# S4D convolution on one core: one table for both sides of the state, and the odd chunk sums as three split products

## The chip, the cores and the metric

One Trainium2 chip, one of its cores. The metric is the device time of one execution in microseconds. The kernel before takes 853.24 us (median of three runs, 852.15 to 855.84).

## The reference, cut to what matters

```python
dtA = (-exp(log_A_real) + 1j * A_imag) * exp(log_dt)[:, None]           # 128 channels x 64 modes
Cs = C * (exp(dtA) - 1.0) / A
K = 2.0 * einsum('hn,hnl->hl', Cs, exp(dtA[:, :, None] * arange(2048))).real
y = irfft(rfft(u * mask) * rfft(K))[..., :2048] + u * mask * D[:, None]  # u: 64 batches x 128 x 2048
x = x + y * mask                                                         # mask: t < length[b]
```

For each channel, 64 sequences of 2048 samples go through a causal convolution whose kernel is a sum of 64 damped complex exponentials. The work is fp32.

## The kernel before

A **prologue** builds tables of powers of the exponentials for all channels. Then comes one **slot per channel**, 128 of them. Slots 0 to 11 and 120 to 127 are written out; the 108 between run in a hardware loop, six to a turn, where semaphore values and table addresses stand in registers. No scheduler places anything: each engine runs its own `slot(g, j)` in the order in which it is written, and semaphores tie the engines together. In slot h, `here` is channel h, `one`, `two` and `three` are h+1, h+2 and h+3, `back` is h-1.

**Per channel.** A sequence is cut into 8 chunks of 256 samples, each an even and an odd block of 128. `turn_x` (L1006) transposes x on TensorE: four transposes for the even blocks into the PSUM bank xt_even, four for the odd ones into xt_odd. ScalarE copies xt_even to `uhi` (rounded to fp32r) and xt_odd to `uod` (full fp32); VectorE forms the remainder `ulo` (`x_low`). `chunk_sums` (L1025 to L1039) gives what each of the first 7 chunks adds to the 128 state rows (64 real, 64 imaginary) for 7 x 64 = 448 columns: three fp32r products for the even block (hi by hi, hi by lo, lo by hi; lines 1021 to 1023) and one fp32 product with `eod` for the odd block (L1038), which the trace shows as two matmuls. It raises `s_in`.

**The scan.** The states follow from the sums by products with powers of the exponential in `RV`. ScalarE writes a copy with the halves swapped (`turn_odds`, `turn_pairs`, `turn_evens`: two ACTIVATEs each into `room`), and VectorE does two instructions for each step (`mid`, then v in place; L911), in `pairs`, `fours` and `odds`. `z_high` on ScalarE and `z_low` on VectorE split the finished states into `zhi` and `zlo`.

**Outputs.** `toep_even` and `toep_odd` (L1067) are the products within a chunk, with the Toeplitz rows `traw` that SyncE's queue reads from the DRAM tensor krows, split by `thi` and `tlo`. `from_state` adds zhi, zlo by the table `fhi`, `flo`, three fp32r products of 256 columns for each of four pieces, and raises `s_y` after the second and the fourth. It waits for `s_zlo` and `s_flo` before the first. `choose` (L900) then writes y into the x tile under the mask, and SyncE's queue stores it.

**Tables E and F.** For each channel, GpSimd's `channel` forms 2 x 256 columns by two products of W and B (L520, L521) and a difference (L529): half 0 is turned by `turn_e` and gives ehi, elo, eod, half 1 gives fhi, flo. W holds two families of powers, X for E and Y for F, both made in the prologue by `level` (six instructions for a doubling) on VectorE.

**The order that matters here.** TensorE: sums of `one`, `turn_x` of `two`, Toeplitz products of `here` with `turn_e` of `two` in the middle, `from_state` of `here`. VectorE: `choose` of `back` twice, `odds` of `here`, `pairs` of `one`, `z_low` of `here`, `x_low` and `e_low` of `two`, `fours` of `one`. So within a slot `z_low(here)` stands behind `pairs(one)`, which waits for the sums of the same slot; and `from_state(here)`, later in that slot, waits for `z_low(here)`.

## Time and profile before

| | us |
|---|---|
| profiled execution, its own time | 853.14 |
| its span, first to last instruction | 851.3 |
| start of the Toeplitz products of slot 0 | 51.4 |
| TensorE busy | 816.7 (96%) |
| VectorE, GpSimd, ScalarE busy | 730.0, 641.3, 619.2 |
| granted TensorE clock, mean | 0.999 |

Busy time is the union of an engine's records. TensorE's records overlap, since a matmul's ends are modelled and the next one streams while it drains: the pace is read from start to start. A row of the timeline gives start, duration, engine, line, operation, what is written and read, how many records are merged, and in brackets the idle time before it with its releaser.

### The profile page before, as it was taken

How to read it: one execution, taken by the hardware profiler on the slowest of the kernel's cores; microseconds unless marked ns; L12 is line 12 of the kernel's file. 1: busy time of each engine (PE TensorE's matmuls, PEld its weight loads, DVE VectorE, ACT ScalarE, POOL GpSimd, SP SyncE). 2: the span in 40 equal slices, each digit the busy share in tenths (PEclk: the TensorE clock that was granted, in tenths of full speed). 3: DMA queues.
4: the chain of work that ended last, by engine and by line, in shares of the span. 5: the costliest groups of instructions: out<-in, count | busy, mean ns of one | idle time of the engine just before them, and what ended most of it. 6: DMA issues, size and time to landing. Idle time of an engine off the chain costs nothing.

```text
span 851.3 us, 22217 instructions
## 1 busy us (share of the span) xinstructions
PE 816.7 (96%) x6168; PEld 752.9 (88%) x6168; DVE 730.0 (86%) x2020; ACT 619.2 (73%) x1717; POOL 641.3 (75%) x708
## 2 busy tenths in 40 slices
PE   0799999999999999999999999999999999999997
PEld 0779998989999999999998999999999999999996
DVE  7878988888888888888888888888888888888886
ACT  4777776777777777777777777777777777777774
POOL 5887776777777878787787878777787877778771
PEclk9999999999999999999999999999999999999999
DMA  5235877777777787777877777777777877777875
GB/s 108 50 74 145 197 189 183 192 186 184 190 187 199 185 193 192 185 197 184 196 185 193 191 186 197 184 195 185 194 191 190 196 184 195 185 194 189 197 191 137
DMA packets 161391, 152.69 MB, mean 179 GB/s; under 512 B 13656, under 2 KB 161240, under 8 KB 161240
## 3 DMA queue, kind: packets, MB, share of 16 engines
q1 hardware_dynamic: 161064, 152.15, 72.5%
q10 hardware_dynamic: 304, 0.26, 0.1%
q8 instruction: 11, 0.18, 0.1%
q14 instruction: 12, 0.10, 0.0%
HBM read 84.02 MB, written 67.30 MB: 178 GB/s over the span
## 4 chain that ended last, share of the span: by engine, by line
PE 89%; DVE 4%; DMA 3%; ACT 1%; SPq 1%; issue 1%; DVEq 0%
PE y L1021 13%; PE y L1023 13%; PE y L1022 13%; PE y L1067 13%; PE v L1038 11%; PE xt_even L1006 6%; PE xt_odd L1006 6%; PE v L1021 3%; PE v L1022 3%; DMA xall<-in_x_dram 3%; PE v L1023 3%; PE y L1016 2%; PE y L1017 2%; SPq L355 1%; ACT room L542 0%
## 5 line engine op out<-in xcount | busy, mean ns | idle before, releaser
L542 ACT ACTIVATE room<-v 64x192 f32<-64x192 f32 (+1 forms) x768 | 235.8, 307 | 171.9 <-DVE v L911 156.0
L911 DVE SCALAR_TENSOR_TENSOR v<-v,RV,mid 128x192 f32<-128x192 f32 (+2 forms) x512 | 192.3, 376 | 55.0
L911 DVE SCALAR_TENSOR_TENSOR mid<-room,RV,v 128x192 f32<-128x192 f32 (+2 forms) x512 | 184.3, 360 | 42.1 <-ACT room L542 23.5
L1021 PE MATMUL y<-thi,uhi 128*128 128x256 f32 x511 | 186.0, 364 | 0.0
L900 DVE COPY_PREDICATED xall<-mask,y 128x512 f32<-128x512 int32 x254 | 174.4, 735 | 1.7 <-issue 1.7
L1021 PE MATMUL y<-fhi,zhi 128*128 128x256 f32 x511 | 154.3, 302 | 1.3 <-DVE zlo L735 1.2
L1023 PE MATMUL y<-thi,ulo 128*128 128x256 f32 x511 | 144.2, 282 | 0.0
L1023 PE MATMUL y<-fhi,zlo 128*128 128x256 f32 x511 | 143.8, 281 | 0.0
L1022 PE MATMUL y<-tlo,uhi 128*128 128x256 f32 x511 | 143.7, 281 | 0.0
L1022 PE MATMUL y<-flo,zhi 128*128 128x256 f32 x511 | 143.7, 281 | 0.0
L521 POOL TENSOR_TENSOR room<-W,B 128x512 f32 (+1 forms) x127 | 141.7, 1116 | 0.0
L520 POOL TENSOR_TENSOR room<-W,B 128x512 f32 (+1 forms) x127 | 134.8, 1061 | 3.0 <-DVE W L873 2.8
L1067 PE MATMUL y<-traw,uod 128*128 128x128 f32 x680 | 130.4, 273 | 0.0
L1006 PEld LDWEIGHTS xt_even<-ident,xall 128*128 128x128 f32 x512 | 63.3, 142 | 56.8 <-issue 46.9
L503 POOL TENSOR_TENSOR flo<-pf,fhi 128x256 fp32r<-128x256 f32 x64 | 46.7, 730 | 79.0 <-ACT fhi L542 79.0
L1067 PEld LDWEIGHTS y<-traw,uod 128*128 128x128 f32 x680 | 104.8, 189 | 0.0
L503 POOL TENSOR_TENSOR flo<-room,fhi 128x256 fp32r<-128x256 f32 x64 | 46.7, 729 | 73.8 <-ACT fhi L542 73.8
L1022 PEld LDWEIGHTS y<-tlo,uhi 128*128 128x128 f32 x511 | 98.1, 192 | 0.2 <-issue 0.2
L1021 PEld LDWEIGHTS y<-thi,uhi 128*128 128x128 f32 x511 | 97.4, 191 | 0.9 <-POOL tlo L508 0.7
L1021 PEld LDWEIGHTS y<-fhi,zhi 128*128 128x128 f32 x511 | 96.5, 189 | 1.7 <-issue 1.7
L1022 PEld LDWEIGHTS y<-flo,zhi 128*128 128x128 f32 x511 | 96.7, 189 | 0.0
L1023 PEld LDWEIGHTS y<-fhi,zlo 128*128 128x128 f32 x511 | 96.5, 189 | 0.0
(195 smaller groups left out, 1939.6 us busy)
## 6 DMA issues: line engine op xcount, KB each, us to landing
xall<-in_x_dram SPq DMA_DIRECT2D x256, 256.0 KB, 4.6
out_dram<-xall SPq DMA_DIRECT2D x254, 256.0 KB, 3.4
traw<-krows SPq DMA_DIRECT2D x128, 128.0 KB, 3.0
NXY<-B SPq DMA_DIRECT2D x2, 512.0 KB, 6.2
krows<-ksb SPq DMA_DIRECT2D x8, 1.0 KB, 2.2
krows<-ksb SPq DMA_DIRECT2D x8, 4.0 KB, 3.6
krows<-ksb SPq DMA_DIRECT2D x8, 11.0 KB, 4.0
out_dram<-xall SPq DMA_DIRECT2D x1, 128.0 KB, 2.5
```

Source lines behind the costliest of these rows:

```text
L503: pool.tensor_tensor(flo[j % 2][:], pf[j % 2][:, 1, ::-1], fhi[j % 2][:].bitcast(F32), ALU.subtract).then_inc(s_flo, 1)
L520: pool.tensor_tensor(tw1[:], w1, b1, ALU.mult).then_inc(s_gpa, 1)
L521: pool.tensor_tensor(tw2[:], w2, b2, ALU.mult).then_inc(s_gpa, 1)
L542: return act.activation(dst, src, ACT.Copy)
L900: dve.copy_predicated(xs[j][:, a:a + 512], mask[:, a:a + 512], yb[j % 2][part][:]).then_inc(s_pred, 1)
L911: return dve.scalar_tensor_tensor(out=out, in0=src, scalar=RV[:, k:k + 1, h], in1=other, op0=ALU.mult, op1=ALU.add)
L1006: mm = pe.transpose(xt[par][:, c * P:(c + 1) * P], xs[j][:, b * BLK:(b + 1) * BLK], ident[:])
L1021: pe.matmul(o, a_hi, b_hi, start=start, stop=False, skip_group_check=True)
L1022: pe.matmul(o, a_hi, b_lo, start=False, stop=False, skip_group_check=True)
L1023: return pe.matmul(o, a_lo, b_hi, start=False, stop=stop, skip_group_check=True)
L1038: pe.matmul(v, eod[k][:], uod[j % 3][:, cols], start=False, stop=True, skip_group_check=True).then_inc(s_in, 1)
L1067: mm = pe.matmul(y_cols(g, j, c)[:, BLK:2 * BLK], uod[j % 3][:, b], traw[k][:, :BLK - 1:-1], start=False, stop=False, skip_group_check=True)
```

## The change

**One table.** The starting values of X and Y are changed so that E and F are the same table: X starts at half the root of the modulus of z = Y(1) times lambda, with its sign and phase; the prologue gets the products for z (GpSimd), two squares and a square root (ScalarE), a reciprocal and five small operations (VectorE). The states are then multiplied by a factor for each mode, kept as a seventh row of `RV` (step S): `z_high` gets a per-partition scale, `z_low` becomes a SCALAR_TENSOR_TENSOR. GpSimd forms 256 columns instead of 512. VectorE's levels are made for Y (levels 0 to 2), then X (0 to 3), then Y's last, where before each of the first three did both; the prologue's transposes go through 3 PSUM banks instead of 5, and ScalarE alone takes them.

**Odd sums.** E is split over its whole width (`ehi`, `elo` with 256 columns). `x_odd` makes a second copy `uoh` (fp32r, 448 columns), GpSimd forms its remainder `uol` (`odd_low`). `chunk_sums` becomes `even_sums` and `odd_sums`, three fp32r products each.

**Order.** On TensorE the sums of `one` have the odd transposes of `two` between them, and the even transposes, now of `three`, stand in the middle of `from_state`. The other engines' slots are reordered as the diff shows. SyncE's queue loads x four slots ahead instead of three and stores before it loads `traw`.

```diff
-BANKS = 5
+BANKS = 3
 
 
 STEPS = [("R", 0), ("R", 1),
-         ("B1", 12), ("B2", 12), ("X1", 12), ("X2", 12), ("Y1", 12), ("Y2", 12),
-         ("B1", 8), ("B2", 8), ("X1", 8), ("X2", 8), ("Y1", 8), ("Y2", 8),
-         ("Y1", 0), ("Y1", 4), ("Y2", 0), ("Y2", 4),
-         ("B1", 0), ("B1", 4), ("B2", 0), ("B2", 4),
-         ("X1", 0), ("X1", 4), ("X2", 0), ("X2", 4)]
+         ("B1", 12), ("B2", 12), ("Y1", 12), ("Y1", 8), ("B1", 8), ("B2", 8),
+         ("X1", 12), ("X2", 12), ("X1", 8), ("X2", 8), ("X1", 0), ("X1", 4), ("X2", 0), ("X2", 4),
+         ("B1", 0), ("B1", 4), ("B2", 0), ("B2", 4), ("Y1", 0), ("Y1", 4), ("S", 0)]
 T_K = len(STEPS)
...
-        W2 = sb("W2", [P, 2, SQ, H])
+        W2 = sb("W2", [P, SQ, H])
...
-        ehi = [sb(f"ehi{i}", [P, P], F32R) for i in range(2)]
-        elo = [sb(f"elo{i}", [P, P], F32R) for i in range(2)]
-        eod = [sb(f"eod{i}", [P, P]) for i in range(2)]
-
-        tw1, tw2 = (room[:, i].rearrange("p (a b c) -> p a b c", a=2, b=SQ) for i in (5, 6))
-        pf = [sb("pf0", [P, 2, CHUNK]), room[:, 7].rearrange("p (a q) -> p a q", a=2)]
+        ehi = [sb(f"ehi{i}", [P, 2 * P], F32R) for i in range(2)]
+        elo = [sb(f"elo{i}", [P, 2 * P], F32R) for i in range(2)]
+        uoh = [sb(f"uoh{i}", [P, EVERY], F32R) for i in range(2)]
+        uol = [sb(f"uol{i}", [P, EVERY], F32R) for i in range(2)]
+
+        tw1, tw2 = (room[:, i, 0:CHUNK].rearrange("p (b c) -> p b c", b=SQ) for i in (5, 6))
+        pf = [sb("pf0", [P, CHUNK])[:], room[:, 7, 0:CHUNK]]
         fhi = [sb(f"fhi{i}", [P, CHUNK], F32R) for i in range(2)]
...
-                start = isinstance(g, int) and g == 0
                 early = isinstance(g, int) and g < 2
-                if exists(g, j, 3) and not (start and j + 3 < SLOTS):
-                    if exists(g, j, -3):
-                        sp.wait_ge(s_out[(j + 3) % SLOTS], 32 * on(g, j, 3)[0])
-                    load_x(*on(g, j, 3))
+                if exists(g, j, 4) and not (early and h + 4 < SLOTS):
+                    sp.wait_ge(s_out[(j + 4) % SLOTS], 32 * on(g, j, 4)[0])
+                    load_x(*on(g, j, 4))
...
+                if exists(g, j, -1):
+                    sp.wait_ge(s_pred, 2 * h)
+                    store(*on(g, j, -1))
                 if exists(g, j, 2):
                     sp.wait_ge(s_intra, h + 1)
                     load_t(*on(g, j, 2))
-                if exists(g, j, -1):
-                    sp.wait_ge(s_pred, 2 * h)
-                    store(*on(g, j, -1))
...
+            def table(g, j):
+
+                h = chan(g, j)
+                w1 = W1[:, 0, h, :].unsqueeze(2).broadcast_to([P, SQ, SQ])
+                w2 = W2[:, :, h].unsqueeze(2).broadcast_to([P, SQ, SQ])
+                b1 = B1[:, h, :].unsqueeze(1).broadcast_to([P, SQ, SQ])
+                b2 = B2[:, h, :].unsqueeze(1).broadcast_to([P, SQ, SQ])
...
+                pool.tensor_tensor(tw1, w1, b1, ALU.mult).then_inc(s_gpa, 1)
+                pool.tensor_tensor(tw2, w2, b2, ALU.mult).then_inc(s_gpa, 1)
...
+            def odd_low(g, j):
+
+                h = chan(g, j)
+                pool.wait_ge(s_uod, h + 1)
+                pool.wait_ge(s_uoh, h + 1)
+                if exists(g, j, -2):
+                    pool.wait_ge(s_in, h - 1)
+                pool.tensor_tensor(uol[j % 2][:], uod[j % 3][:, 0:EVERY], uoh[j % 2][:].bitcast(F32),
+                                   ALU.subtract).then_inc(s_uol, 1)
...
+                f_low(*here)
+                if not exists(g, j, -1):
+                    t_low(*here)
+                if has2 and exists(g, j, -1):
+                    difference(*two)
+                if has1:
+                    odd_low(*one)
+                if has2 and not exists(g, j, -1):
+                    difference(*two)
+                if exists(g, j, -1):
+                    t_low(*here)
+                if has3:
+                    table(*three)
...
+                if exists(g, j, -2):
+                    act.wait_ge(s_in, chan(g, j) - 1)
+                copy(uoh[j % 2][:], xt[1][:, 0:EVERY]).then_inc(s_uoh, 1)
...
+            act.wait_ge(s_z, 1)
+            act.activation(sq_re, z_re, ACT.Square)
+            act.activation(sq_im, z_im, ACT.Square).then_inc(s_sq, 1)
...
+            take(("B1", 12), ("Y1", 12))
+            act.wait_ge(s_n2, 1)
+            act.activation(m0, n2, ACT.Sqrt).then_inc(s_m0, 1)
...
-                copy(ehi[j % 2][:], e_bank(j)[:, 0:P]).then_inc(s_ehi, 1)
-
-            def e_odd(g, j):
-                copy(eod[j % 2][:], e_bank(j)[:, P:2 * P]).then_inc(s_eod, 1)
+                copy(ehi[j % 2][:], e_bank(j)).then_inc(s_ehi, 1)
...
-                copy(zhi[j % 2][:, B:], vb[j % 2][:, B:NC * B]).then_inc(s_zhi, 1)
+                act.activation(zhi[j % 2][:, B:], vb[j % 2][:, B:NC * B], ACT.Copy,
+                               scale=RV[:, 6:7, chan(g, j)]).then_inc(s_zhi, 1)
...
-                if has0:
-                    turn_evens(*here)
-                if has1 and not first:
-                    f_high(*one)
+                three, has3 = on(g, j, 3), exists(g, j, 3)
+                turn_evens(*here)
                 if has1:
                     turn_odds(*one)
-                if has1:
                     if isinstance(g, int) and g == 0 and 1 <= j <= 4:
                         k_copy(j)
                     t_high(*one)
-                if has0:
-                    z_high(*here)
-                if has2 and has0:
-                    x_high(*two)
+                z_high(*here)
+                if has1:
+                    f_high(*one)
+                    turn_pairs(*one)
+                if has2:
                     e_high(*two)
-                    e_odd(*two)
-                if has1:
-                    turn_pairs(*one)
-                if has2 and has0:
                     x_odd(*two)
-
...
-            link(level(dve, link, both, coarse[0], temps, 0))
+            link(level(dve, link, y_table, coarse[0], temps, 0))
             powers(R_POW, NPOW, [(lim, sn), (lre, cs)])
-            level(dve, link, both, coarse[1], temps, 1).then_inc(s_nxy, 1)
-            dve.wait_ge(s_nxy, 1)
-            level(dve, link, both, coarse[2], temps, 2).then_inc(s_nxy, 1)
-            dve.wait_ge(s_nxy, 2)
-            level(dve, link, y_table, coarse[3], temps, 3).then_inc(s_nxy, 1)
-            dve.wait_ge(s_nxy, 3)
-            level(dve, link, x_table, coarse[3], temps, 3).then_inc(s_nxy, 1)
+            level(dve, link, y_table, coarse[1], temps, 1).then_inc(s_ny, 1)
+            dve.wait_ge(s_sq, 1)
+            dve.scalar_tensor_tensor(out=n2, in0=sq_re, scalar=1e-30, in1=sq_im, op0=ALU.max, op1=ALU.add).then_inc(s_n2, 1)
+            dve.wait_ge(s_ny, 1)
+            level(dve, link, y_table, coarse[2], temps, 2).then_inc(s_ny, 1)
+
+            dve.tensor_scalar(pos, z_re, 0.0, None, ALU.is_ge)
+            dve.wait_ge(s_m0, 1)
+            link(dve.reciprocal(inv, m0))
+            link(dve.scalar_tensor_tensor(out=inv, in0=n2, scalar=0.25, in1=inv, op0=ALU.mult, op1=ALU.mult))
+            dve.scalar_tensor_tensor(out=u0, in0=m0, scalar=0.25, in1=inv, op0=ALU.mult, op1=ALU.add)
+            link(dve.scalar_tensor_tensor(out=u1, in0=pos, scalar=0.5, in1=z_re, op0=ALU.subtract, op1=ALU.mult))
+            dve.scalar_tensor_tensor(out=NXY[:, SQ - 1, 0, 1, :], in0=pos, scalar=0.5, in1=z_im,
+                                     op0=ALU.subtract, op1=ALU.mult)
+            link(dve.tensor_tensor(NXY[:, SQ - 1, 0, 0, :], u0, u1, ALU.add))
+            link(level(dve, link, x_table, coarse[0], temps, 0))
+            for k in range(1, 4):
+                level(dve, link, x_table, coarse[k], temps, k).then_inc(s_nx, 1)
+                dve.wait_ge(s_nx, k)
+            dve.wait_ge(s_ny, 2)
+            level(dve, link, y_table, coarse[3], temps, 3).then_inc(s_ny, 1)
...
-                less(zlo[j % 2][:, B:], vb[j % 2][:, B:NC * B], zhi[j % 2][:, B:]).then_inc(s_zlo, 1)
+                dve.scalar_tensor_tensor(out=zlo[j % 2][:, B:], in0=vb[j % 2][:, B:NC * B], scalar=RV[:, 6:7, chan(g, j)],
+                                         in1=zhi[j % 2][:, B:].bitcast(F32), op0=ALU.mult,
+                                         op1=ALU.subtract).then_inc(s_zlo, 1)
...
-                if not has1:
-                    odds(*here)
-                if hasb:
+                if has1:
+                    e_low(*one)
+                fours(*here)
+                if hasb and has1:
+                    dve.wait_ge(s_y, 2 * h - 1)
+                    choose(*back, 0)
+                sixth(*here)
+                if hasb and has1:
+                    dve.wait_ge(s_y, 2 * h)
+                    choose(*back, 1)
+                odds(*here)
+                if hasb and not has1:
                     dve.wait_ge(s_y, 2 * h - 1)
                     choose(*back, 0)
                     dve.wait_ge(s_y, 2 * h)
                     choose(*back, 1)
-                if has0 and has1:
-                    odds(*here)
                 if has1:
                     pairs(*one)
-                if has0:
-                    z_low(*here)
-                if has2 and has0:
+                z_low(*here)
+                if has2:
                     x_low(*two)
-                    e_low(*two)
                 if has1:
-                    fours(*one)
+                    fours_turned(*one)
...
-            def chunk_sums(g, j):
+            def even_sums(g, j):
 
                 h, k = chan(g, j), j % 2
                 cols = slice(0, EVERY)
-                v = vb[k][:, B:NC * B]
                 pe.wait_ge(s_uhi, h + 1)
                 pe.wait_ge(s_elo, h + 1)
                 pe.wait_ge(s_ulo, h + 1)
                 if exists(g, j, -2):
                     pe.wait_ge(s_zlo, h - 1)
-                three(v, ehi[k][:], elo[k][:], uhi[j % 3][:, cols], ulo[j % 3][:, cols], True, False)
-                pe.wait_ge(s_eod, h + 1)
+                three(vb[k][:, B:NC * B], ehi[k][:, 0:P], elo[k][:, 0:P], uhi[j % 3][:, cols], ulo[j % 3][:, cols],
+                      True, False)
+
+            def odd_sums(g, j):
+
+                h, k = chan(g, j), j % 2
                 pe.wait_ge(s_uod, h + 1)
-                pe.matmul(v, eod[k][:], uod[j % 3][:, cols], start=False, stop=True,
-                          skip_group_check=True).then_inc(s_in, 1)
+                pe.wait_ge(s_uol, h + 1)
+                three(vb[k][:, B:NC * B], ehi[k][:, P:2 * P], elo[k][:, P:2 * P], uoh[k][:], uol[k][:],
+                      False, True).then_inc(s_in, 1)
 
...
-                first = isinstance(g, int) and g == 0 and j == 0
-                if has1 and not first:
-                    chunk_sums(*one)
-                if has2 and not first:
-                    turn_x(*two, 0)
+                if has1:
+                    even_sums(*one)
+                if has2:
                     turn_x(*two, 1)
+                if has1:
+                    odd_sums(*one)
                 if isinstance(g, int) and g == 0 and 1 <= j <= 4:
                     pe.wait_ge(s_pred, 2 * j - 1)
                     k_rest(j)
                 if isinstance(g, int) and g == 0 and 2 <= j <= 5:
                     pe.wait_ge(s_ksb, j - 1)
-                if has0:
-                    for c in range(2):
-                        toep_even(*here, c)
-                        toep_odd(*here, c)
-                if has2 and has0:
+                for c in range(2):
+                    toep_even(*here, c)
+                    toep_odd(*here, c)
+                if has2:
                     turn_e(*two)
-                if has0:
-                    for c in range(2, CPH):
-                        toep_even(*here, c)
-                        toep_odd(*here, c)
-                    for c in range(CPH):
-                        from_state(*here, c)
+                for c in range(2, CPH):
+                    toep_even(*here, c)
+                    toep_odd(*here, c)
+                for c in range(2):
+                    from_state(*here, c)
+                if exists(g, j, 3):
+                    turn_x(*on(g, j, 3), 0)
+                for c in range(2, CPH):
+                    from_state(*here, c)
```

TensorE's queue from the last product of one slot to the first Toeplitz product of the next (v holds the sums, xt the transposes, y the outputs); before:

```order
L1023 MATMUL y<-fhi,zlo 128x256
L1021 MATMUL v<-uhi,ehi 128x448
L1022 MATMUL v<-ulo,ehi 128x448
L1023 MATMUL v<-uhi,elo 128x448
L1038 MATMUL v<-uod,eod 128x448
L1006 MATMUL xt_even<-ident,xall 128x128 x4
L1006 MATMUL xt_odd<-ident,xall 128x128 x4
```

and now, the same place:

```order
L1095 MATMUL y<-fhi,zlo 128x256
L1093 MATMUL v<-uhi,ehi 128x448
L1094 MATMUL v<-ulo,ehi 128x448
L1095 MATMUL v<-uhi,elo 128x448
L1078 MATMUL xt_odd<-ident,xall 128x128 x4
L1093 MATMUL v<-uoh,ehi 128x448
L1094 MATMUL v<-uol,ehi 128x448
L1095 MATMUL v<-uoh,elo 128x448
```

Before, eight transposes stand between the sums and the Toeplitz products that follow; now none do.

VectorE's queue in a slot of the loop, from `pairs` to `x_low` (ISA and REGISTER_ALU work out addresses and semaphore values; an ISA in front of an operation carries its wait); before:

```order
L911 SCALAR_TENSOR_TENSOR mid<-room,RV,v 128x192
L911 ISA
L911 SCALAR_TENSOR_TENSOR v<-v,RV,mid 128x3x64
L735 TENSOR_TENSOR zlo<-v,zhi 128x448
L738 REGISTER_ALU
L735 TENSOR_TENSOR ulo<-xt_even,uhi 128x512
L735 TENSOR_TENSOR elo<-y,ehi 128x128
```

and now:

```order
L963 SCALAR_TENSOR_TENSOR mid<-room,RV,v 128x192
L963 ISA
L963 SCALAR_TENSOR_TENSOR v<-v,RV,mid 128x3x64
L1008 ISA
L1008 SCALAR_TENSOR_TENSOR zlo<-v,RV,zhi 128x448
L778 REGISTER_ALU
L775 TENSOR_TENSOR ulo<-xt_even,uhi 128x512
```

`z_low` still stands behind `pairs`, reads RV and has an ISA in front of it that waits for `zhi`; `fours` has moved on, around the two halves of `choose`; `e_low` too.

ScalarE's queue around the same place of the loop, from the swapped copies to `zhi`; before, then now:

```order
L542 ACTIVATE room<-v 64x192 x2
L653 REGISTER_ALU
L542 ACTIVATE fhi<-pf 128x256
L542 ACTIVATE room<-v 64x192 x2
L657 ISA
L542 ACTIVATE thi<-traw 128x256
L542 ACTIVATE zhi<-v 128x448
```

```order
L588 ACTIVATE room<-v 64x192 x4
L705 ISA
L588 ACTIVATE thi<-traw 128x256
L727 ISA
L727 ACTIVATE zhi<-v,RV 128x448
```

`fhi` no longer stands between `turn_evens` and `turn_odds` (now four ACTIVATEs in a row); `thi` still stands between `turn_odds` and `zhi`.

## Rows read from the trace of the kernel before

**Rows 1.** Timeline of TensorE, one slot of the loop (start us, us):

```profile
402.91 0.37 PE L1021 MATMUL v<-uhi,ehi 128*128 128x448 f32 x1
...
403.52 0.91 PE L1038 MATMUL v<-uod,eod 128*128 128x448 f32 x2
404.27 0.60 PE L1006 MATMUL xt_even<-ident,xall 128*128 128x128 f32 x4
404.71 0.60 PE L1006 MATMUL xt_odd<-ident,xall 128*128 128x128 f32 x4
405.06 0.36 PE L1021 MATMUL y<-thi,uhi 128*128 128x256 f32 x1
...
407.60 0.37 PE L1021 MATMUL y<-fhi,zhi 128*128 128x256 f32 x1
...
409.11 0.37 PE L1021 MATMUL v<-uhi,ehi 128*128 128x448 f32 x1
```

**Rows 2.** Timeline of ScalarE, the same slot:

```profile
404.59 0.66 ACT L542 ACTIVATE room<-v 64x192 f32<-64x192 f32 x2
...
405.60 0.53 ACT L542 ACTIVATE zhi<-v 128x448 fp32r<-128x448 f32 x1
```

**Rows 3.** Timeline of VectorE, the same slot:

```profile
405.39 0.41 DVE L911 SCALAR_TENSOR_TENSOR mid<-room,RV,v 128x192 f32<-128x192 f32 x1
405.95 0.42 DVE L911 SCALAR_TENSOR_TENSOR v<-v,RV,mid 128x192 f32<-128x192 f32 x1
406.28 0.61 DVE L735 TENSOR_TENSOR zlo<-v,zhi 128x448 fp32r<-128x448 f32 x1
```

**Rows 4.** Timeline of all engines in slot 126, which has no transposes:

```profile
837.27 0.91 PE L1038 MATMUL v<-room,eod 128*128 128x448 f32 x2
...
838.22 0.66 ACT L542 ACTIVATE room<-v 64x192 f32<-64x192 f32 x2 [0.27 <-PE v L1038]
...
839.79 0.62 DVE L735 TENSOR_TENSOR zlo<-v,zhi 128x448 fp32r<-128x448 f32 x1
...
840.56 0.35 PE L1021 MATMUL y<-fhi,zhi 128*128 128x256 f32 x1
```

**Rows 5.** Timeline of ScalarE in the prologue, a copy without and with a scale:

```profile
25.39 0.49 ACT L542 ACTIVATE RV<-v 128x384 f32<-128x384 f32 x1 [1.12 <-PE v L1131]
25.97 0.58 ACT L596 ACTIVATE RV<-v,sgn 128x384 f32<-128x384 f32 x1
```

**Rows 6.** Groups of VectorE by line and shape, 200 to 800 us (busy, mean ns):

```profile
L735 DVE TENSOR_TENSOR zlo<-v,zhi 128x448 fp32r<-128x448 f32 x97 | 59.5, 613 | 0.0
...
L911 DVE SCALAR_TENSOR_TENSOR mid<-room,RV,v 128x192 f32<-128x192 f32 x194 | 78.7, 406 | 0.0
...
L735 DVE TENSOR_TENSOR elo<-y,ehi 128x128 fp32r<-128x128 f32 x97 | 27.1, 279 | 0.0
```

**Rows 7.** Timeline of GpSimd, `t_low` of the slot of rows 1:

```profile
406.94 0.73 POOL L508 TENSOR_TENSOR tlo<-traw,thi 128x256 fp32r<-128x256 f32 x1
```

**Rows 8.** Waits of TensorE's weight loads, 100 to 800 us (total, times, longest):

```profile
PEld xt_even L1006 <- DMA xall<-in_x_dram: 8.3, 18, 1.7
```

**Rows 9.** Timeline of VectorE in the prologue, the first instruction of three levels:

```profile
23.23 0.42 DVE L288 TENSOR_TENSOR xt_even<-NXY,y 128x256 f32<-128x256 f32 x1
...
25.45 0.70 DVE L288 TENSOR_TENSOR xt_even<-NXY,y 128x512 f32<-128x512 f32 x1
...
29.29 0.70 DVE L288 TENSOR_TENSOR xt_even<-NXY,y 128x512 f32<-128x512 f32 x1
```

**Rows 10.** Timeline of ScalarE in the prologue, a table load and two copies:

```profile
11.03 1.28 ACT L570 ACT_TABLE_LOAD   x1
...
30.17 1.09 ACT L542 ACTIVATE B<-y 128x512 f32<-128x512 f32 x2 [2.58 <-PE y L1131]
```

**Rows 11.** Timeline of TensorE: warm-up transposes, first kernel matmul, first Toeplitz matmul:

```profile
25.73 3.62 PE L998 MATMUL y<-ident 128*128 128x128 f32 x16
...
42.28 0.48 PE L1144 MATMUL v<-B,W 64*128 64x128 f32 x2
...
51.41 0.39 PE L1021 MATMUL y<-thi,uhi 128*128 128x256 f32 x1
```

254 lines of the change are left out of this document (134 added, 120 removed).

## The prediction

> **What bounds the kernel now.** I read the table of busy time first (TensorE 96%), then TensorE's timeline over one slot of the loop, then that of the engines which feed it. TensorE has no gap there: a slot runs from 402.91 to 409.11 us, 6.20 us, every matmul starting where the one before leaves off [rows 1]. The three fp32r products of the sums take 0.61 us, the fp32 product of the odd block 0.75 (403.52 to 404.27), the eight transposes 0.79, the Toeplitz products with turn_e 2.54, from_state 1.51 [rows 1].
>
> What the reader is to see next is how close the second limit lies: **a chain that begins and ends on TensorE within one slot**. The sums raise s_in; ScalarE makes the swapped copies (404.59), VectorE does pairs (405.39, 405.95) and then z_low (406.28, ended 406.89), and only then may from_state start [rows 2, 3]. It started at 407.60, and a start can follow the end of z_low by 0.15 (840.41 to 840.56 [rows 4]), so the slack is 407.60 - 406.89 - 0.15 = 0.56 us a slot. That is less than the 0.79 of the transposes, which stand inside this chain's window.
>
> **The change part by part.** The sum is made against the profiled execution, 853.14 us, which is the median to 0.1.
>
> *TensorE's own work.* Three fp32r products of 448 columns take the place of one fp32 product: 0.61 for 0.75 [rows 1]. There is one more change from fp32 back to fp32r. The first matmul behind fp32 work starts 0.09 early (four transposes followed by transposes take 0.44, followed by a matmul 0.35 [rows 1]) and gives that back at once, so a change costs nothing that the rows show. Laid end to end, the new slot is 0.61 (even sums) + 0.35 (four transposes) + 0.70 (odd sums, with the 0.09) + 2.45 (Toeplitz and turn_e, no longer behind transposes, so 2.54 - 0.09) + 0.79 + 0.35 + 0.79 (from_state in halves around four transposes) = 6.04 us. Were nothing else in the way, 0.16 a slot would be won.
>
> *The window.* s_in now comes behind odd_sums, and no transposes follow: four were moved ahead, four into from_state. From the end of the sums to from_state TensorE has 2.45 us of work where it had 0.79 + 2.54 = 3.33 [rows 1].
>
> *The chain.* Counted from the same point: the last record of the sums ends 0.16 behind the next start (403.52 + 0.91 against 404.27 [rows 1]); ScalarE starts 0.04 later, where it is free (838.18 to 838.22 [rows 4]). Before, it was busy with f_high and began only at 404.59 [rows 2]; f_high now stands elsewhere, which gives 0.12 back. From the swapped copies to zhi is 1.01 (404.59 to 405.60 [rows 2]), with t_high between, as now. zhi itself takes 0.53 [rows 2] and gets a scale that is read per partition: a copy of 384 columns takes 0.49 without and 0.58 with one [rows 5], so 0.62. Then z_low. In the loop an operation behind an instruction that works out an address starts 0.15 after what it waits for (405.80 to 405.95 [rows 3]); the order shows that z_low gets such an instruction, with the wait on it: 0.15. z_low becomes a SCALAR_TENSOR_TENSOR: the line through 279 ns at 128 and 613 at 448 gives 346 at 192 columns, where a SCALAR_TENSOR_TENSOR takes 406 [rows 6], so 0.61 + 0.06 = 0.67. Then 0.15 to TensorE [rows 4]. Sum: 0.16 + 0.04 + 1.01 + 0.62 + 0.15 + 0.67 + 0.15 = **2.80 us**. The way over pairs is shorter: 0.20 + 0.66 + 0.15 + 0.41 + 0.15 + 0.33 + 0.67 + 0.15 = 2.72 [rows 2, 3, 4]; zhi comes last.
>
> So TensorE **waits 2.80 - 2.45 = 0.35 us before from_state in every slot**, and a loop slot takes 6.04 + 0.35 = 6.39 us. Nobody else can take the time up: the next sums stand behind from_state in TensorE's queue. Slot 126 shows the new arrangement in the old kernel: no transposes follow its sums, and from_state starts 840.56 - 838.02 = 2.54 behind their end (837.27 + 0.75) [rows 1, 4], with a plain copy, a TENSOR_TENSOR and waits on constants. That is 0.26 below my 2.80, and 0.09 for the scale, 0.06 for z_low and 0.11 for the address instruction make it up.
>
> *Sum over slots.* The loop's 108 slots: 108 x (6.39 - 6.20) = +20.5. In the 20 that are written out the wait on constants saves 0.11: 6.28, so +0.08 in sixteen, and in slots 1 to 4, where the kernel's own matmuls (k_rest) stand between sums and Toeplitz products and cover the wait, -0.16: together +0.7.
>
> *Moved and covered.* GpSimd gets odd_low, 448 columns at between 0.73 (that of 256 [rows 7]) and 448/256 of it, 1.28; its products and difference are halved. It now has two things that TensorE needs soon: uol before odd_sums, tlo before the Toeplitz products. uoh is ready about 0.6 us before the slot's end (swapped copies for fours, e_high, uod and uoh follow zhi on ScalarE), so uol at 0.6 and tlo at 1.3 us of the slot, wanted at 0.8 and 1.5. A delay of tlo would lie inside the 0.35 anyway. VectorE: e_low and z_low grow by 0.13 and 0.06 [rows 6]; it ends z_low at 4.2 us, so x_low, fours and both halves of choose are done 1.3 us into the next slot, where turn_e wants the second at 2.8. Those I cost at nothing; without this cover 0.2 to 0.3 a slot. SyncE's queue stores ahead of traw, but traw waits for the end of the Toeplitz products in either order, which is the later wait: nothing. Loading x a slot earlier takes away waits for it, 8.3 us at the weight loads, 18 times [rows 8]; weight loads run ahead of the matmuls by up to 0.2, so 8.3 - 3.6 = 4.7 at most and none at least: -3.
>
> *Prologue.* VectorE's level of 512 elements takes 3.84 (25.45 to 29.29), of 256 2.22 (23.23 to 25.45) [rows 9]; on a straight line 1.4 for 128 and 1.0 for 64. Before, the last of two levels of 512 ended at 29.29 + 2 x 3.84 = 37.0. Now X can't start before the square root. The warm-up began at 25.73 and B was copied from 30.17 on [rows 10, 11]; with eight transposes of x ahead (+0.79) and Y's first level alone (-0.4) B comes at 30.6, three takes of 0.55 [rows 10] make 32.2, a table load 1.28 [rows 10] 33.5, the root 33.9. Small operations of about 0.25 make 35.6, X's levels 1.0 + 1.4 + 2.2 + 3.84 = 44.1, Y's last 48.0. ScalarE has a copy and ten takes behind X: 44.1 + 0.6 + 5.5, then 0.6 for b0 and the handover: 50.8, where the first kernel matmul stood at 42.28 [rows 11]. That path (krows, traw, slot 0 at 51.41 [rows 11]) is the one that ends last in the prologue, so **+8.6**; I bound it by +5 and +12.
>
> The Trainium skill (ScalarE: Activation LUTs, What ACT_TABLE_LOAD costs) puts a table switch at 2.66 us with the drain that follows. No row here shows how soon an ACTIVATE may follow a load. By the page the root would come 1.4 later and the total would be 1.4 higher.
>
> *Total:* 853.1 + 20.5 + 0.7 + 8.6 - 3 = **880 us**.
>
> **Rivals.** *A, the chain fits and TensorE stays the bound:* 124 slots x -0.16 = -19.8, +8.6, -3: 839 us, faster. For it: 96% busy, and 0.56 of slack today. Against: the window loses 0.88, and slot 126 needed 2.54 even in the cheap form. It decides if the chain is below 2.45. Chance 0.12.
> *B, the chain is the bound but my additions to it are too dear:* with scale and z_low at nothing, pairs comes last: 2.72 - 0.06 = 2.66, a wait of 0.21, 6.25 a slot: 853.1 + 5.4 - 1 + 8.6 - 3 = 863 us. Chance 0.17.
> *C, GpSimd is late as well:* odd_low runs at 1.28 or more and starts only after uoh, so odd_sums waits ahead of the chain; 0.2 to 0.3 a slot on top, 27 us: 907 us, from the point at which uol comes later than 0.8 us into the slot. Against: 0.2 of slack by the rows. Chance 0.08.
> *D, the change doesn't do what it says:* the products cost as much as the fp32 one (0.14 a slot more than I say, 898 us) or the prologue overlaps better (871). Chance 0.05.
>
> **How the numbers follow.** My case has 0.58 and gives 880, with 0.1 us a slot either way (about 11 us) and the prologue's bounds. The range takes in B and stops before C and A: 859 to 893. What a measurement of this kernel can tell from no change is about 0.5%, 849 to 857.5. Faster is A, 0.12; within it, the low end of B, 0.05; slower 0.83.
>
> **What would show it.** A gap before fhi,zhi in every loop slot with VectorE's zlo as its releaser, 0.35 long, and 6.39 from one even sum to the next; three products of the odd sums in 0.70; zhi at 0.62 and zlo at 0.67; the first Toeplitz product at 60. If the gap is missing, A holds and the chain was mis-sized; if GpSimd's uol is the releaser, C.

## The result, and the profile after

The changed kernel takes **972.24 us** (median of four runs, 969.11 to 974.97) against 852.99 us: a ratio of 1.139, 95% interval 1.134 to 1.144. The forecast was 880 us, 859 to 893. The direction was right, the size was not: +119 us where the sum had +27. The profiled execution has a span of 971.7 us.

The page of the changed kernel, busy time and the chain that ended last:

```profile
PE 836.0 (86%) x6281; PEld 794.9 (82%) x6281; DVE 759.9 (78%) x2041; ACT 669.3 (69%) x1720; POOL 605.3 (62%) x843
DMA 54%; SPq 29%; issue 7%; DVE 4%; PE 3%; ACT 2%; POOL 0%; DVEq 0%; ACTq 0%; POOLq 0%
DMA out_dram<-xall 53%; SPq L361 18%; SPq L366 10%; DMA traw<-krows 1%; SPq L378 1%; PE v L1209 1%; SPq L422 0%; ACT room L588 0%; PE y L1093 0%; PE v L1093 0%; ACT zhi L727 0%; DVE zlo L1008 0%; ACT B L588 0%; PE y L1095 0%; PE y L1094 0%
```

No engine bounds this kernel. The chain of waits goes through SyncE's queue (SPq) and the landing of the stores: landings of stores (53%), issues of x (L361, 18%) and issues of stores (L366, 10%) make up 81% of the span. My sum had given that queue one clause, "nothing".

The waits of the loop (200 to 900 us), of all engines and then of SyncE's queue; columns are engine, line, what it waited for, us in total, times, longest:

```profile
PE y L1093 <- DVE zlo L1008: 76.5, 95, 2.0
ACT thi L588 <- DMA traw<-krows: 69.3, 94, 1.9
DVE zlo L1008 <- ACT zhi L727: 65.4, 93, 1.9
```
```profile
SPq L361 <- DMA out_dram<-xall: 261.0, 99, 3.5
SPq L373 <- PE y L1141: 0.3, 1, 0.3
```

The same view of the kernel before, SyncE's queue at 200 to 800 us:

```profile
SPq L362 <- PE y L1067: 195.0, 97, 2.3
```

Before, the queue's only wait was at traw, for the last Toeplitz product, 97 times in 97 slots. After, it waits at the x load for a store's landing, every slot, and at traw practically never: by the time the queue comes to traw, the Toeplitz products are over. So traw is issued late, ScalarE waits for it at thi, z_high stands behind thi, z_low behind z_high, from_state behind z_low. The gap of [rows 2, 3]'s chain did appear before from_state, with zlo as its releaser as forecast, but with a mean of 0.8 us a slot and for another reason.

SyncE's queue over one and a half slots of the changed kernel:

```profile
444.53 1.51 SPq L361 DMA_DIRECT2D xall<-in_x_dram  x2
446.26 1.51 SPq L366 DMA_DIRECT2D out_dram<-xall  x2
448.04 0.68 SPq L373 DMA_DIRECT2D traw<-krows  x1
451.81 1.53 SPq L361 DMA_DIRECT2D xall<-in_x_dram  x2
453.63 1.48 SPq L366 DMA_DIRECT2D out_dram<-xall  x2
455.67 0.50 SPq L373 DMA_DIRECT2D traw<-krows  x1
```

This is a **cycle that closes on itself**. x is loaded four slots ahead into six tiles, so slot h loads into the tile of channel h-2, which slot h-1 has stored. The load stands first in the queue and waits until that store has landed; this slot's own store stands behind it. One turn is the issue of x (1.53), a gap (0.29), the issue of the store (1.48) and some 3.8 us from there over its landing to the next issue of x (the median of 200 to 900 us; 4.0 in the rows above): 7.1 us. From the first sums of channel 13 to those of channel 120 a slot takes 7.11 us on average; before it took 6.22.

What of the 119 us lies where: 107 intervals of the loop x (7.11 - 6.22) = 96; slot 0's first Toeplitz product at 66.83 instead of 51.41 us [rows 11], 15; the rest, some 9, in the slots that are written out.

### The profile page after: what moved, and what is told of

It reads as the page before. It is cut to its first block, busy times and chain, and to the rows that moved or that the text cites. A ratio compares the mean times of both kernels' runs of the same rounds, so it can differ in the third digit from the quotient of the medians.

```text
span 971.7 us, 22927 instructions
## 1 busy us (share of the span) xinstructions
PE 836.0 (86%) x6281; PEld 794.9 (82%) x6281; DVE 759.9 (78%) x2041; ACT 669.3 (69%) x1720; POOL 605.3 (62%) x843
## 4 chain that ended last, share of the span: by engine, by line
DMA 54%; SPq 29%; issue 7%; DVE 4%; PE 3%; ACT 2%; POOL 0%; DVEq 0%; ACTq 0%; POOLq 0%
DMA out_dram<-xall 53%; SPq L361 18%; SPq L366 10%; DMA traw<-krows 1%; SPq L378 1%; PE v L1209 1%; SPq L422 0%; ACT room L588 0%; PE y L1093 0%; PE v L1093 0%; ACT zhi L727 0%; DVE zlo L1008 0%; ACT B L588 0%; PE y L1095 0%; PE y L1094 0%
## 5 line engine op out<-in xcount | busy, mean ns | idle before, releaser
L1093 PE MATMUL y<-fhi,zhi 128*128 128x256 f32 x511 | 164.8, 323 | 92.2 <-DVE zlo L1008 91.7
L952 DVE COPY_PREDICATED xall<-mask,y 128x512 f32<-128x512 int32 x254 | 190.4, 750 | 2.4 <-issue 2.4
L1093 PE MATMUL y<-thi,uhi 128*128 128x256 f32 x511 | 176.1, 345 | 0.0
L1008 DVE SCALAR_TENSOR_TENSOR zlo<-v,RV,zhi 128x448 fp32r<-128x448 f32 x128 | 87.5, 684 | 82.3 <-ACT zhi L727 81.4
L588 ACT ACTIVATE thi<-traw 128x256 fp32r<-128x256 f32 x128 | 53.4, 417 | 84.5 <-DMA traw<-krows 84.0
L557 POOL TENSOR_TENSOR uol<-uod,uoh 128x448 fp32r<-128x448 f32 x85 | 98.4, 1158 | 17.4 <-issue 14.1
```

The source lines that it names most:

```text
L557: pool.tensor_tensor(uol[j % 2][:], uod[j % 3][:, 0:EVERY], uoh[j % 2][:].bitcast(F32), ALU.subtract).then_inc(s_uol, 1)
L588: return act.activation(dst, src, ACT.Copy)
L952: dve.copy_predicated(xs[j][:, a:a + 512], mask[:, a:a + 512], yb[j % 2][part][:]).then_inc(s_pred, 1)
L1008: dve.scalar_tensor_tensor(out=zlo[j % 2][:, B:], in0=vb[j % 2][:, B:NC * B], scalar=RV[:, 6:7, chan(g, j)], in1=zhi[j % 2][:, B:].bitcast ...
L1093: pe.matmul(o, a_hi, b_hi, start=start, stop=False, skip_group_check=True)
```

## The experiments

All times are medians, ratios are to the kernel before, run on the same chip (852.4 to 854.6 us). "Slot" is the mean in the loop, between the first even sums of channels 13 and 120.

### Is it the queue? The changed kernel without it

e1_x_last, the changed kernel with the x load moved to the end of SyncE's slot:

```diff
-                if exists(g, j, 4) and not (early and h + 4 < SLOTS):
-                    sp.wait_ge(s_out[(j + 4) % SLOTS], 32 * on(g, j, 4)[0])
-                    load_x(*on(g, j, 4))
                 if exists(g, j, -1):
                     sp.wait_ge(s_pred, 2 * h)
                     store(*on(g, j, -1))
                 if exists(g, j, 2):
                     sp.wait_ge(s_intra, h + 1)
                     load_t(*on(g, j, 2))
+                if exists(g, j, 4) and not (early and h + 4 < SLOTS):
+                    sp.wait_ge(s_out[(j + 4) % SLOTS], 32 * on(g, j, 4)[0])
+                    load_x(*on(g, j, 4))
```

> The changed kernel, with one edit: in SyncE's slot the load of x (four ahead) stands last, behind the store and the load of traw, instead of first. Theory (the queue's cycle): a tile is stored in slot h-1 and reloaded in slot h, so each slot holds a store's landing (about 3.9 us behind its second issue), two issues of x (1.8 with the gap) and two of the store (1.5) one after the other, 7.1 us, and traw stands behind them. With the x load last its wait has long been met, so the slot falls to what my chain of sums and zhi gives: 6.39 us, a wait of 0.35 before from_state, no wait of thi for traw: about 107 x 0.72 = 77 and a few us of the first slots less, 888 us. Rival (the chain itself is longer than I said, or the memory system is slower in this order): over 940 us, with zlo still 0.8 late.

Measured: 889.67 us (ratio 1.044, 1.042 to 1.046), slot 6.39. Moving three lines takes 82.6 of the 119 us away. What is left is what I had forecast. In e1, TensorE's last product of traw, from_state's first, and the engines that it waits for:

```profile
403.01 0.39 PE L1141 MATMUL y<-traw,room 128*128 128x128 f32 x2
403.50 0.36 PE L1093 MATMUL y<-fhi,zhi 128*128 128x256 f32 x1
```
```profile
401.91 0.62 ACT L727 ACTIVATE zhi<-v,RV 128x448 fp32r<-128x448 f32 x1
```
```profile
402.67 0.68 DVE L1008 SCALAR_TENSOR_TENSOR zlo<-v,RV,zhi 128x448 fp32r<-128x448 f32 x1
```

Where from_state waits for nothing it follows the traw product by 0.14 (so in e3, below); here it follows by 0.49: a wait of 0.35. zhi takes 0.62, z_low starts 0.14 behind its end and takes 0.68, from_state starts 0.15 later. These are the terms of the forecast to within 0.01.

### Is it only the queue? The kernel before with it, and its two ingredients apart

e2_before_sp is the kernel before with SyncE's slot of the changed kernel (x four ahead and first, then store, then traw), nothing else:

```diff
-                if exists(g, j, 3) and not (start and j + 3 < SLOTS):
-                    if exists(g, j, -3):
-                        sp.wait_ge(s_out[(j + 3) % SLOTS], 32 * on(g, j, 3)[0])
-                    load_x(*on(g, j, 3))
+                if exists(g, j, 4) and not (early and h + 4 < SLOTS):
+                    sp.wait_ge(s_out[(j + 4) % SLOTS], 32 * on(g, j, 4)[0])
+                    load_x(*on(g, j, 4))
...
+                if exists(g, j, -1):
+                    sp.wait_ge(s_pred, 2 * h)
+                    store(*on(g, j, -1))
                 if exists(g, j, 2):
                     sp.wait_ge(s_intra, h + 1)
                     load_t(*on(g, j, 2))
-                if exists(g, j, -1):
-                    sp.wait_ge(s_pred, 2 * h)
-                    store(*on(g, j, -1))
```

> The kernel before, with only SyncE's slot of the changed kernel: x four slots ahead, the store before traw. Theory (the queue's cycle): it alone is enough to hold a slot at about 7.1 us in the old kernel too, which has nothing else of the change: 853 + 107 x 0.9 = 949 us, with waits of thi for traw. Rival (the late traw only hurts because of the new order on the other engines): within 1% of 853.

Measured: 956.89 us (1.123, 1.120 to 1.126), slot 7.07; the queue waits for out_dram 221.7 us in 85 slots of 200 to 800. The queue alone does it to the old kernel as well.

The slot of SyncE was changed in two ways: x is loaded one slot further ahead, and the store goes ahead of traw. e5_x_three puts back only the first, in the changed kernel:

```diff
-                if exists(g, j, 4) and not (early and h + 4 < SLOTS):
-                    sp.wait_ge(s_out[(j + 4) % SLOTS], 32 * on(g, j, 4)[0])
-                    load_x(*on(g, j, 4))
+                if exists(g, j, 3) and not (early and h + 3 < SLOTS):
+                    sp.wait_ge(s_out[(j + 3) % SLOTS], 32 * on(g, j, 3)[0])
+                    load_x(*on(g, j, 3))
```

> The changed kernel (972.2 us) with one number put back: SyncE's queue loads x three slots ahead, as in the kernel before, still as the first thing of its slot and with the store still ahead of traw. Theory (the stall needs the tile that was stored only one slot earlier: x four ahead into six tiles): the tile of channel h-3 was stored in slot h-2 and has landed, no wait for out_dram at the x load, a slot 6.39 us, total about 890 as in run e1_x_last (889.7). Rival (the store ahead of traw is what delays traw, so x three or four ahead is the same): 950 to 972.

e11_x_four is the opposite: the kernel before, its order of x, traw and store kept, with the first seven lines of e2's diff alone: x four ahead instead of three.

> The kernel before (853.2 us) with one number changed: SyncE's queue loads x four slots ahead instead of three; its order (x, traw, store) stays. Theory (a cycle in one in-order queue: store issue 1.5, landing 3.8, x issue 1.6, and here traw's issue and its gap, 0.6, in it as well): a slot takes 7.5 us instead of 6.2, total 990 to 1010, slower than run e2_before_sp (956.9), where traw stood outside. Rival (four ahead is harmless, the order of store and traw did it): 853.

Measured: e5 890.62 us (1.043, 1.041 to 1.045), slot 6.40. e11 990.22 us (1.159, 1.157 to 1.162), slot 7.33. SyncE's queue in e11:

```profile
443.46 1.49 SPq L350 DMA_DIRECT2D xall<-in_x_dram  x2
445.21 0.39 SPq L362 DMA_DIRECT2D traw<-krows  x1
445.89 1.52 SPq L355 DMA_DIRECT2D out_dram<-xall  x2
450.45 1.49 SPq L350 DMA_DIRECT2D xall<-in_x_dram  x2
```

So the queue's part of the loss, some 82 of the 119 us, hangs on the distance of four together with the load's place, first in its slot: either alone put right brings 890. The store ahead of traw is harmless by itself (e5); with four ahead it even helps, since traw's issue is then outside the cycle (7.07 against 7.33 us).

### The chain on TensorE: what the window is worth

e3_turn_behind is e1 with the odd transposes behind odd_sums instead of ahead of them, which puts 0.35 us of TensorE's work back into the window:

```diff
-                if has2:
-                    turn_x(*two, 1)
                 if has1:
                     odd_sums(*one)
+                if has2:
+                    turn_x(*two, 1)
```

> e1 and one more edit: TensorE's four odd transposes stand behind odd_sums instead of ahead of it. Theory (the chain from the sums to from_state is 2.80 against 2.45 of work): the window grows by 0.44 to 2.89, the wait of 0.35 goes, a slot takes 6.04 to 6.10 unless GpSimd's uol, now wanted 0.35 earlier, is late by up to 0.15: 0.29 to 0.35 a slot less than e1, 31 to 37 us, about 854. Rival (TensorE is held by something else): as e1.

e4_zhi_first is e1 with t_high behind z_high on ScalarE, which shortens the chain instead:

```diff
-                    t_high(*one)
                 z_high(*here)
                 if has1:
+                    t_high(*one)
```

> e1 and one other edit: on ScalarE t_high stands behind z_high instead of ahead of it. Theory: zhi comes 0.33 earlier, but then pairs comes last: 2.72 against 2.45, a wait of 0.27 where e1 has 0.35: 0.08 a slot less, about 8 us less than e1. If zhi alone were the last (my additions for pairs too high), the wait would fall to near nothing: 37 us less.

Measured: e3 866.84 us (1.016, 1.014 to 1.018), slot 6.20 (median 6.17); e4 880.31 us (1.031, 1.029 to 1.033), slot 6.31. e4 gave its 0.08 a slot. e3's wait before from_state is gone, but its slot was 0.1 longer than expected and the total 13 us too high. The odd sums wait for uol: in the mean slot from 200 to 800 us they start 0.05 late, and behind that gap their first product takes 0.28 from start to start instead of 0.20, together 0.12. Without it TensorE's work is about 6.05 (sums and transposes 1.57, Toeplitz part 2.53, from_state with its transposes 1.95), close to the 6.04 of the forecast; the shortest slots of e9_cycle, below, have just that. ScalarE and GpSimd of e3 around that wait, and TensorE's odd sums of the same slot:

```profile
399.48 0.55 ACT L588 ACTIVATE uoh<-xt_odd 128x448 fp32r<-128x448 f32 x1
```
```profile
400.16 1.16 POOL L557 TENSOR_TENSOR uol<-uod,uoh 128x448 fp32r<-128x448 f32 x1 [0.17 <-issue]
```
```profile
401.47 0.44 PE L1093 MATMUL v<-uoh,ehi 128*128 128x448 f32 x1
402.15 0.60 PE L1078 MATMUL xt_odd<-ident,xall 128*128 128x128 f32 x4
```

This is a second cycle: the odd sums (0.68 from start to start, and 0.16 more to the end of the last record), ScalarE from the swapped copies to the end of uoh (3.85), GpSimd's odd_low (1.16) and three hand-overs give 6.17 us. e9_cycle takes f_high out of it (e3 as the base):

```diff
                 if has1:
-                    f_high(*one)
                     turn_pairs(*one)
                 if has2:
                     e_high(*two)
                     x_odd(*two)
+                if has1:
+                    f_high(*one)
```

and puts GpSimd's slot in another order, with `odd_low(0, 1)` ahead of slot 0:

```diff
-                f_low(*here)
-                if not exists(g, j, -1):
-                    t_low(*here)
-                if has2 and exists(g, j, -1):
-                    difference(*two)
-                if has1:
+                if has1 and exists(g, j, -1):
                     odd_low(*one)
-                if has2 and not exists(g, j, -1):
-                    difference(*two)
-                if exists(g, j, -1):
-                    t_low(*here)
+                t_low(*here)
+                f_low(*here)
+                if has2:
+                    difference(*two)
```

> The kernel of run e3_turn_behind (866.8 us) with f_high moved behind x_odd on ScalarE, and GpSimd's slot in the order odd_low, t_low, f_low, difference, table (odd_low(0,1) ahead of the loop). In e3 a slot takes 6.17 us where TensorE's work is 6.12: the odd sums wait 0.05 for uol, over a cycle of odd sums, ScalarE (3.85 us to the end of uoh), odd_low 1.16. Theory: without f_high in it the cycle is 0.35 shorter, the slot 6.12 (TensorE the bound, as in the kernel before with 6.19), and slot 0 gains 2 us since odd_low no longer stands behind t_low: 866.8 - 6 - 2 = 858.8. Rival (GpSimd's difference is now late for turn_e in the middle of the Toeplitz products, ready at 403.6 where it is wanted at 403.7): a new wait there, slot 6.2 or more, 866 or slower.

Measured: 855.72 us (1.003, 1.002 to 1.005), slot 6.11 (median 6.10, many at 6.04 to 6.05). 11 us less than e3, 3 better than expected. The wait for uol is gone, and the shortest slots show TensorE's work without waits, 6.04 and not the 6.12 of the expectation. So e9's mean slot isn't TensorE's bound: the rival is in it as well, with a mean gap at turn_e that is 0.04 us above its smallest.

### The prologue

Up to the first kernel matmul e3's prologue is the changed kernel's, and its times agree within 0.1 us, so three edits of e3 take it apart. First the rows of the changed kernel itself: VectorE behind the square root, GpSimd over the same time, ScalarE's table load.

```profile
33.71 0.31 DVE L903 SCALAR_TENSOR_TENSOR root<-root 128x64 f32<-128x64 f32 x1
34.05 1.19 DVE L904 SCALAR_TENSOR_TENSOR root<-root 128x64 f32<-128x64 f32 x1
35.16 0.21 DVE L905 SCALAR_TENSOR_TENSOR root<-root 128x64 f32<-128x64 f32 x1
35.41 1.18 DVE L906 SCALAR_TENSOR_TENSOR NXY<-root 128x64 f32<-128x64 f32 x1
36.51 1.30 DVE L908 TENSOR_TENSOR NXY<-root 128x64 f32<-128x64 f32 x1
```
```profile
33.90 1.26 POOL L297 TENSOR_TENSOR xall<-room,lre 128x512 f32<-128x512 f32 x1
35.24 1.27 POOL L298 TENSOR_TENSOR room<-xall 128x512 f32<-128x512 f32 x1
36.47 1.26 POOL L299 TENSOR_TENSOR room<-xall 128x512 f32<-128x512 f32 x1
```
```profile
31.54 1.28 ACT L657 ACT_TABLE_LOAD   x1
32.83 0.26 ACT L657 ACTIVATE root<-root 128x64 f32<-128x64 f32 x1
```

Three operations of 64 columns take six times what their neighbours take. Each ends within 0.1 us of the end of a GpSimd instruction (35.16, 36.51, 37.73), and the short one, at 35.16, fell between two of them.

e6_root_psum gives these operations one operand in PSUM:

```diff
+        p_pos, p_u1 = (yb[0][1][:, CHUNK + i * N:CHUNK + (i + 1) * N] for i in range(2))
+        p_inv = yb[1][0][:, CHUNK:CHUNK + N]
...
+            dve.tensor_scalar(p_pos, z_re, 0.0, None, ALU.is_ge)
...
-            dve.scalar_tensor_tensor(out=u0, in0=m0, scalar=0.25, in1=inv, op0=ALU.mult, op1=ALU.add)
-            link(dve.scalar_tensor_tensor(out=u1, in0=pos, scalar=0.5, in1=z_re, op0=ALU.subtract, op1=ALU.mult))
+            dve.scalar_tensor_tensor(out=u0, in0=m0, scalar=0.25, in1=p_inv, op0=ALU.mult, op1=ALU.add)
+            link(dve.scalar_tensor_tensor(out=p_u1, in0=p_pos, scalar=0.5, in1=z_re, op0=ALU.subtract, op1=ALU.mult))
...
```

> The kernel of run e3_turn_behind (866.8 us) with one edit in the prologue: the small VectorE operations behind the square root read one of their two inputs from PSUM instead of both from SBUF (one TENSOR_SCALAR of 64 columns more). In e3 three of them took 1.19, 1.18 and 1.30 us for 64 columns and each ended where a TENSOR_TENSOR of GpSimd ended (35.08, 36.42, 37.65). Theory (an operation of VectorE with two SBUF inputs waits for GpSimd's instruction): they take 0.2 to 0.3 each, X's levels end at 43.5 us instead of 46.3, total 864.0. Rival (they are slow because of their form, or of what ScalarE writes beside them): the durations stay, 866.8. Second rival (X's levels are not what ends last in the prologue): durations fall and the total stays at 866.8.

e7_root_early moves the square root on ScalarE:

```diff
+            act.wait_ge(s_n2, 1)
+            act.activation(m0, n2, ACT.Sqrt).then_inc(s_m0, 1)
             take(("B1", 12), ("Y1", 12))
-            act.wait_ge(s_n2, 1)
-            act.activation(m0, n2, ACT.Sqrt).then_inc(s_m0, 1)
```

> The kernel of run e3_turn_behind (866.8 us) with the square root and its table load ahead of the three copies of B and Y on ScalarE. The sum of squares is ready at 27.25 us and VectorE is free from 29.5, but the root came at 33.0. Theory (the root's place in ScalarE's order sets the start of X's levels): table load 27.3 to 28.6, root at 28.9, first small operation at 29.5 instead of 33.04, X's levels end at 42.8 instead of 46.3, first kernel matmul at 51.5 instead of 55.06, total 863.3. Rival (B's and Y's copies, now later or unchanged at 29.8, hold TensorE and GpSimd, and the path goes by them): less than 1 us, 866.

e8_warm fills TensorE's gaps:

```diff
+            def warm_before(step, n):
+
+                t = STEPS.index(step)
+                pe.wait_ge(s_free[t % BANKS], t // BANKS)
+                keep_warm(n, pro[t % BANKS])
...
+            warm_before(("B1", 8), 24)
             pe.wait_ge(s_bdup, 2)
             turn(("B1", 8), ("B2", 8))
+            warm_before(("X1", 12), 12)
...
+            warm_before(("X1", 0), 12)
             pe.wait_ge(s_nx, 3)
```

> The kernel of run e3_turn_behind (866.8 us) with 24, 12 and 12 idle transposes on TensorE in its three gaps of the prologue (31.1 to 35.6, 37.5 to 40.3, 44.3 to 46.3 us), into the bank that is free next. In e3 the profile shows the lower clock there, four transposes take 1.06 instead of 0.60 us by the record and one copy starts every 0.85 us. Theory (the half clock sets the pace of the ten copies behind X's levels): four transposes in 0.60, a copy every 0.60 to 0.65, first kernel matmul 2 to 2.5 us earlier, total 864.5. Rival (the pace is ScalarE's copy and its hand-over with three banks): a copy still every 0.85, total 866.8.

Measured, against e3's 866.84: e6 862.86 (ratio to before 1.011, 1.009 to 1.013), e7 862.57 (1.012, 1.010 to 1.014), e8 863.80 (1.013, 1.010 to 1.016). By the medians they took 4.0, 4.3 and 3.0 us off. But e3 ran on another chip; by the ratios to the kernel before, each on its own chip, it is 3.9, 3.2 and 2.2, against 2.8, 3.5 and 2.3 expected. Each of these differences is uncertain by 2 to 3 us, so e8's gain in the total isn't clear of noise; what each edit does is read from its trace. In e7 X's levels ended at 43.7 us, not at 42.8: there four of the small operations were held, for 1.19 to 1.30 us each. The same operations in e6:

```profile
34.49 0.22 DVE L907 SCALAR_TENSOR_TENSOR root<-root,y 128x64 f32<-128x64 f32 x1
34.62 0.23 DVE L908 SCALAR_TENSOR_TENSOR y<-y,root 128x64 f32<-128x64 f32 x1
34.88 0.23 DVE L909 SCALAR_TENSOR_TENSOR NXY<-y,root 128x64 f32<-128x64 f32 x1
35.02 0.21 DVE L911 TENSOR_TENSOR NXY<-root,y 128x64 f32<-128x64 f32 x1
```

GpSimd ran the same instructions beside them, at 1.27 us each. So the long times were waits for GpSimd by instructions that read both inputs from SBUF. This is what the Trainium skill says (SBUF — State Buffer, Who interferes with whom): an instruction of VectorE with two SBUF inputs contends with a GpSimd instruction that reads SBUF, over a shared port pair that it calls an exclusive lock. The traces agree, with 1.18 to 1.30 us against 0.21 to 0.23.

TensorE of e3, four transposes behind X's last level, and the same place in e8:

```profile
48.10 1.06 PE L1209 MATMUL y<-ident,NXY 128*128 128x128 f32 x4
48.95 1.06 PE L1209 MATMUL v<-ident,NXY 128*128 128x128 f32 x4
```
```profile
48.51 0.60 PE L1209 MATMUL y<-ident,NXY 128*128 128x128 f32 x4
48.94 0.63 PE L1209 MATMUL v<-ident,NXY 128*128 128x128 f32 x4
```

The granted clock in 40 slices of the span, of e3 and of e8:

```profile
PEclk9779999999999999999999999999999999999999
```
```profile
PEclk9999999999999999999999999999999999999999
```

In e3 it was 0.7 in the second and third slice (22 to 65 us), a mean that holds stretches at 1.2 GHz (1.06 us for four transposes) behind gaps of up to 4.4 us; in e8, with the gaps filled, four transposes take 0.60 as at 2.4 GHz. Six of the ten copies behind X's levels came 0.85 us apart in e3 and 0.47 to 0.58 in e8: from the end of X's levels to the first kernel matmul 8.8 us became 6.7, which is what the forecast had for that stretch.

### All of it together, and where its gain went

e10_all is e9 with the edits of e6, e7 and e8.

> Edits of e6_root_psum, e7_root_early, e8_warm and e9_cycle together, on top of e3_turn_behind: x loads last in SyncE's slot, odd transposes behind the odd sums, f_high out of ScalarE's cycle, root early and its operations partly in PSUM, TensorE kept busy in the prologue. If the gains add (against e3's 866.8: 11.1, 4.0, 4.3, 3.0 measured; the cores of the last three act on one path of the prologue, worth 2.8, 3.0 and 2.1 by the traces): 855.7 - 7.9 = 847.8 us, a ratio of 0.993 to 0.994 to the kernel before. Rival (once the root is early, B's levels on GpSimd and the copies of B hold the prologue): 851 to 853, no difference to before.

Measured: 855.25 us (1.0012, 0.9999 to 1.0025): 0.5 us less than e9 by the medians and 1.7 by the ratios, where 8 were expected. The prologue did its part: slot 0's Toeplitz products start at 56.47 us instead of 66.64. But the loop's slot rose from 6.11 to 6.18 us, 7.5 us in 107 intervals. The waits of e10's loop that e9's has less of (2.3, 1.6 and none there):

```profile
ACT thi L586 <- DMA traw<-krows: 13.1, 40, 0.8
DVE zlo L1008 <- ACT zhi L725: 10.1, 30, 0.8
PE y L1093 <- DVE zlo L1008: 1.2, 3, 0.5
```

I took this for traw sharing the DMA engines with the x load right behind it. e12_x_between is e10 with x between the store and traw:

```diff
                 if exists(g, j, -1):
                     sp.wait_ge(s_pred, 2 * h)
                     store(*on(g, j, -1))
-                if exists(g, j, 2):
-                    sp.wait_ge(s_intra, h + 1)
-                    load_t(*on(g, j, 2))
                 if exists(g, j, 4) and not (early and h + 4 < SLOTS):
                     sp.wait_ge(s_out[(j + 4) % SLOTS], 32 * on(g, j, 4)[0])
                     load_x(*on(g, j, 4))
+                if exists(g, j, 2):
+                    sp.wait_ge(s_intra, h + 1)
+                    load_t(*on(g, j, 2))
```

> The kernel of run e10_all (855.25 us, where 848 was expected) with one edit in SyncE's slot: x, four slots ahead, is loaded between the store and traw instead of behind traw. In e10 the prologue's gain arrived (slot 0's Toeplitz products at 56.47 us against 66.64 in e9_cycle), but the loop's mean slot was 6.18 us against 6.11, and ScalarE waited for traw's landing 13.1 us in 40 slots of the stretch 200 to 800 (2.3 us in 8 in e9); traw is issued at 448.04 and x's two loads right behind it, 448.67 to 450.2. Theory (traw shares the DMA engines with the x load issued right behind it and lands late): with x issued 2 us ahead of traw, traw lands earlier than the 3.8 us of e10, the waits for it go, mean slot 6.06 to 6.11, total 847 to 849. Rival 1 (the slots above 6.05 have another cause, DMA engines 80% busy whatever the order): 855. Rival 2 (the x load now stands in front of traw and waits for the store that came one slot earlier, as in the changed kernel): 5.1 us from that store's issue to its landing, 7.7 us to the x load, so no wait; if it does, slots of 7 us and 950.

Measured: 925.16 us (1.083, 1.081 to 1.085), slot 6.80. The theory fell, and neither rival was right. The queue of e12:

```profile
446.52 1.51 SPq L368 DMA_DIRECT2D out_dram<-xall  x2
448.23 1.59 SPq L363 DMA_DIRECT2D xall<-in_x_dram  x2
450.01 0.48 SPq L375 DMA_DIRECT2D traw<-krows  x1
```

The x load does not wait, but traw is issued right behind it, 3.5 us after the store, which itself waits for choose. Landing times, the DMA view at 200 to 800 us (issues, KB, median us to landing), of the kernel before, of e10 and of e12:

```profile
traw<-krows SPq DMA_DIRECT2D x97, 128.0 KB, 3.0
```
```profile
traw<-krows SPq DMA_DIRECT2D x98, 128.0 KB, 3.8
```
```profile
traw<-krows SPq DMA_DIRECT2D x89, 128.0 KB, 4.6
```

In these four kernels traw's landing goes by how closely it follows the issue ahead of it in the queue: before, that one ended 2.4 us earlier (449.11 to 451.55) and traw landed in 3.0; in e10 1.8 (446.22 to 448.04) and 3.8; in the changed kernel 0.3 (447.77 to 448.04) and 4.5; in e12 0.2 and 4.6. The other kernels fit in the main: with 1.6 to 1.8 us between the two (e1, e3 to e9, e13, e14; medians of 200 to 800) traw landed in 3.3 to 3.8, with 0.2 (e2, e11) in 4.5 and 4.1. But at the same distance it differs by up to 0.5, so this isn't all, and no run varied it alone: the cause is not shown. With 4.6 us, ScalarE waits for traw in 75 of 89 slots.

The other way out is to make the landing matter less. ScalarE's t_high stood ahead of z_high, though the first reader of thi, GpSimd's t_low, starts only some 4 us behind z_high (439.71 to 443.67 in e10). e13_t_late is e10, and e14_t_late_old_prologue is e9, with

```diff
                 if has1:
-                    t_high(*one)
                 z_high(*here)
...
                 if has1:
+                    t_high(*one)
                     f_high(*one)
```

> The kernel of run e10_all (855.25 us) with t_high moved on ScalarE from ahead of z_high to behind x_odd. In e10 ScalarE waited for traw's landing with z_high, and so z_low and from_state, behind it (wait for traw 13.1 us, VectorE's zlo for zhi 10.1 us in the stretch 200 to 800), while thi is wanted only 2.5 us later. Theory (traw's landing, held into the chain by t_high's place, makes e10's slots 6.18 us instead of 6.05): with slack of about 2.5 us for it every slot takes 6.05 to 6.07, 110 x 0.12 = 13 us less: 842 us. Rival (the DMA engines, 75 to 80% busy, hold the loop at one slot in 6.1 or more whatever waits for them, so that a faster prologue is given back): 850 to 855.

> The kernel of run e9_cycle (855.72 us) with t_high behind x_odd on ScalarE: e13 without the three edits of the prologue. The difference of the two tells what the prologue is worth once the loop doesn't swallow it. Theory: slots as in e13 (6.05 to 6.07; 6.11 in e9), about 850.5 us, and e13 below it by the 8 us that the traces give (slot 0's Toeplitz products at 56.47 against 66.64 us, of which slots 1 to 11 give back 2). Rival (the loop catches up with whatever the prologue does, since it is bound by something that both share): e13 and e14 within 2 us of each other.

Measured: e13 **849.52 us** (0.9943, 0.9926 to 0.9961), e14 857.14 us (1.0033, 1.0019 to 1.0048). e13 is faster than the kernel before, by 0.6%, and the only one that is. No wait for traw is left in its loop. But it came out 7.5 us above its theory, and e14, at 857, is no better than e9: the slots of e13 and e14 are 6.15 and 6.14. In e13 the gap before from_state has shrunk by the 0.08 us a slot that e10 had there, and 0.04 of it has come back at the even transposes in the middle of from_state. What these wait for can be read from the landings in the trace: from 200 to 800 us eleven of 98 start 0.12 us late or more, the latest 0.44, and in every one of the eleven x's load had landed 0.12 us before, while the other thing that they wait for, VectorE's x_low, had been done for 0.6 us or more. So the next limit is x's landing, by the median 0.24 us ahead of its transposes in e13 and 0.45 in e9. The rest of what lies above 6.04 is the gap at turn_e, 0.04 as in e9. The question that the pair was for is answered: with the same loop, slot 0's Toeplitz products start at 57.73 us in e13 and 64.27 in e14, 6.5 apart, and the spans end 848.6 to 855.6, 7.0 apart (the medians 7.6). What the prologue loses stays lost to the end; the loop gives nothing of it back. Why e10's loop, with the same lines as e9's, met more late traws than e9's stays open: traw followed the issue ahead of it by 1.7 us in both, and landed in 3.5 in e9 and 3.8 in e10.

## Why the forecast was wrong

**The queue: the step that failed.** The forecast said of SyncE: "traw waits for the end of the Toeplitz products in either order, which is the later wait: nothing". It looked at traw's own wait and at the order of store and traw, and both are harmless (e5). It did not ask what stands first in the queue and for what that waits. It did treat x a slot earlier, but only as a gain, "takes away waits for it". The wait on `s_out` was in the diff, next to the tile number; with six tiles and four ahead the tile is that of the store one slot before. A warning stood in SyncE's timeline of the kernel before, which I had not shown:

```profile
445.76 1.51 SPq L355 DMA_DIRECT2D out_dram<-xall  x2
447.56 1.55 SPq L350 DMA_DIRECT2D xall<-in_x_dram  x2
451.55 0.34 SPq L362 DMA_DIRECT2D traw<-krows  x1
```

Both halves of a store have landed there 4.4 us after the start of the first one's issue (median of 200 to 800). With the issue of x (1.5), the gap (0.3) and 0.2 from the landing to the next issue (3.8 less 3.65 in the changed kernel), a turn of the cycle comes to 6.4 us, no shorter than the 6.39 of the forecast's slot. That is the danger and not yet its size: in the changed kernel the store landed after 5.1 us, which makes 7.1, and this wasn't to be read from the kernel before. By e1, the step was worth 82.6 of the 92 us by which the forecast missed; e1's 889.67 us, without it, is 10 above the sum.

**TensorE's chain: right.** 2.80 us against a window of 2.45, a wait of 0.35, a slot of 6.39: e1 has 0.35 and 6.39. zhi 0.62 (0.62), z_low 0.67 (0.68), start behind zhi 0.15 (0.14), odd sums 0.70 (0.69), TensorE without waits 6.04 (e1: 6.39 less 0.35; the shortest slots of e9: 6.04). That pairs comes next, 0.08 lower, is what e4 gave. Rival B (6.25) and A (TensorE the bound) fall. C, GpSimd's uol late, was no part of the result, since the chain hid it; the term was real, though: odd_low took 1.16, near the dear end of its bounds, and it showed as soon as e3 had freed the chain, at 0.12 and not 0.2 to 0.3 a slot. The forecast had not seen the cycle through uoh at all.

**The prologue: the mechanism right, three terms too small.** +15.4 where I had +8.6 (its own terms, 50.8 less 42.28, give 8.5) and a bound of +12. The root came at 33.1 (33.9 forecast), and the table load held the ACTIVATE behind it by no more than its own 1.28 us: the 1.4 of drain that the Trainium skill (ScalarE: Activation LUTs, What ACT_TABLE_LOAD costs) would have added isn't there. The small operations took 4.7 us instead of 1.7 (33.12 to 37.85), since three of them waited for GpSimd; X's levels took the 8.5 us that the line through [rows 9] gives; the copies up to the first kernel matmul took 8.8 instead of 6.7, at TensorE's lower clock; from there to slot 0's first Toeplitz product 11.7 us passed instead of 9.1, mostly because odd_low(0, 1) stood behind t_low on GpSimd and because of the clock. -0.8 + 3.0 + 2.1 + 2.6 is the 6.9 us by which 60 became 66.8. e13 against e14 says that 7.6 us of the prologue could be had back without touching what it computes.

**The saving on x's waits** (-3) came. In e1 the mean slot is the median, 6.39 us, where before the mean lay above it, 6.22 to 6.19: 107 x 0.03 = 3. That this was x's waits fits the trace of e1, which has none for x's landing, but no run took them away alone. The profiled execution of e1 lies 35.4 us above that of the kernel before: 14.4 of it stands ahead of slot 0's Toeplitz products (65.78 against 51.41), 18.6 in the loop and 2.4 in the slots that are written out, where the forecast had 8.6, 20.5 - 3 and 0.7.

**The range** took in the bounds of every term that I had priced, and nothing for the one that I hadn't. A step costed at "nothing" needs the widest bound when a queue is reordered.

## What to carry to other kernels

When loads run ahead into a ring of buffers, count the slots between a buffer's store and its reload, and lay out one turn of the in-order queue: issue, landing, issue. If that turn, with the reload ahead of the next store, is longer than the slot, the queue sets the pace whatever the engines do. Here it was enough to move the load behind what doesn't depend on it (e1, 889.67 us), or to load one slot less ahead (e5, 890.62).

An edit that frees one limit should be followed to the next: here the queue, the chain over z_low and the cycle over uol lay at 7.1, 6.39 and 6.17 us a slot, and turn_e, traw's landing and x's landing between 6.1 and 6.2, and each hid the ones behind it.

## What I had not expected of the hardware

- An instruction of VectorE with both inputs in SBUF, 64 columns of fp32, took 1.18 to 1.30 us beside GpSimd's 1.26-us instructions and 0.21 to 0.23 with one input in PSUM (e6).
- The landing of a 128-KB load (traw) was 3.0 us in the kernel before, at 178 GB/s over the span, and 4.5 in the changed one, at 156: it was longer where less was moved. In the kernels run here it was longer where another issue stood just ahead; that this is the cause isn't shown.
- An ACTIVATE with a new function started 0.01 us after the end of its ACT_TABLE_LOAD. The Trainium skill (ScalarE: Activation LUTs, What ACT_TABLE_LOAD costs) has 1.38 us of drain on top; the measurement decides, and here and in e7 it is not there.
